# Eight copies of each row of combine weights in memory, and one broadcast transfer for a pair of experts in place of two

## What is computed

```python
logits = x @ router_w.T + expert_bias[None, :]
probs = jax.nn.sigmoid(logits)
top_w, top_idx = jax.lax.top_k(probs, TOP_K)                     # 8 of 160
top_w = top_w / (jnp.sum(top_w, axis=-1, keepdims=True) + 1e-09) * 2.5
combine = zeros((T, 160)).at[jnp.arange(T)[:, None], top_idx].set(top_w)
h1 = jax.nn.silu(jnp.einsum('th,eih->eti', x, w_gate))           # 64 inner columns per expert
h1w = h1 * combine.T[:, :, None]
routed = jnp.einsum('eti,ehi->th', h1w, w_down)
shared = jax.nn.silu(x @ w_gate_shared.T) @ w_down_shared.T
```

## Time and profile before

| what | value |
|---|---|
| median of three runs | 459.23 us (458.0 to 460.93) |
| span of the profiled execution | 459.5 us |
| TensorE busy (matmuls) | 403.9 us, 88% |
| VectorE busy | 332.0 us, 72% |
| ScalarE busy | 305.0 us, 66% |
| GpSimd busy | 239.6 us, 52% |
| moved by SyncE's DMA queue | 77.43 MB, 62.4% of 16 engines' span |
| moved by GpSimd's DMA queue | 10.50 MB, 9.1% |

### The profile page before, as it was taken

How to read it: one execution, slowest core, us unless ns; L and a number is a source line. 1 busy time by engine, 2 the same in 40 slices (tenths; PEclk the granted TensorE clock), 3 DMA queues, 4 the chain that set the end, 5 groups by cost and what they waited for, 6 DMA issues and landing times.

```text
span 459.5 us, 8303 instructions
## 1 busy us (share of the span) xinstructions
PE 403.9 (88%) x2271; PEld 314.5 (68%) x2271; DVE 332.0 (72%) x680; ACT 305.0 (66%) x549; POOL 239.6 (52%) x286
## 2 busy tenths in 40 slices
PE   5876789999999999698999999996999998989973
PEld 3556577878778788476777777775866766666742
DVE  5999879877878899665544444444587978898864
ACT  3258835777768778455666666665468978888861
POOL 2689038877787874133333333200056887888810
PEclk8599989999999999978999999999999999999977
DMA  7100378999989999944564554543999999999932
GB/s 230 51 0 7 91 199 234 273 267 265 258 261 267 258 265 260 303 154 156 163 160 141 150 149 141 142 125 85 344 246 240 238 234 242 242 246 240 219 84 68
DMA packets 46330, 88.37 MB, mean 192 GB/s; under 512 B 17170, under 2 KB 21522, under 8 KB 46292
## 3 DMA queue, kind: packets, MB, share of 16 engines
q1 hardware_dynamic: 40004, 77.43, 62.4%
q0 software_dynamic: 6144, 10.50, 9.1%
q10 hardware_dynamic: 144, 0.00, 0.0%
HBM read 77.79 MB, written 10.10 MB: 191 GB/s over the span
## 4 chain that ended last, share of the span: by engine, by line
PE 42%; DVE 17%; ACT 12%; issue 10%; DMA 10%; POOL 4%; SPq 2%; DVEq 2%; ACTq 2%
PE ps L1496 18%; PE ps L1509 12%; DVE arena L1267 7%; ACT arena L865 7%; PE ps L1518 6%; DMA arena<-combine_scratch 4%; POOL arena L647 3%; DVE ps L1054 2%; PE ps L1666 2%; DMA arena<-expert_rows,row_idx 2%; DMA xn<-combine_scratch 2%; PE ps L1629 1%; DVEq L1267 1%; POOL w_lo L630 1%; DMA x_sb<-x 1%
## 5 line engine op out<-in xcount | busy, mean ns | idle before, releaser
L781 ACT ACTIVATE ps<-ps 128x1024 f32<-128x1024 f32 x80 | 80.9, 1011 | 48.0 <-PE ps L1496 38.7
L1060 DVE TENSOR_TENSOR g_lo<-ps,g_hi 128x1024 fp32r<-128x1024 f32 x81 | 98.3, 1214 | 1.3 <-ACT g_hi L794 1.3
L794 ACT ACTIVATE g_hi<-ps 128x1024 fp32r<-128x1024 f32 x81 | 82.8, 1022 | 15.0 <-DVE ps L1054 12.3
L647 POOL DMA_INDIRECT arena<-expert_rows,row_idx x64 | 61.5, 961 | 58.4 <-issue 57.8
L639 POOL DMA_INDIRECT dispatched<-xn,row_idx x64 | 62.2, 971 | 35.9 <-DVE row_idx L1117 19.0
L1267 DVE COPY arena<-ps 128x128 f32 x112 | 32.7, 292 | 56.8 <-ACT arena L865 43.6
L1054 DVE TENSOR_TENSOR ps<-ps,arena 128x1024 f32<-128x1024 f32 x44 | 54.2, 1232 | 22.2 <-ACT ps L781 12.9
L630 POOL TENSOR_TENSOR w_lo<-w_raw,w_hi 128x384 fp32r<-128x384 f32 x52 | 53.8, 1057 | 29.8 <-ACT w_hi L810 24.0
L1496 PE MATMUL ps<-h_hi,w_hi 128*128 128x512 f32 x162 | 54.3, 416 | 10.7 <-DVE g_lo L1060 5.8
L1509 PE MATMUL ps<-g_hi,w_hi 128*128 128x512 f32 x162 | 53.7, 414 | 5.6 <-ACT g_hi L794 4.6
L1518 PE MATMUL ps<-g_lo,w_hi 128*128 128x512 f32 x162 | 52.8, 408 | 3.9 <-DVE g_lo L1060 3.9
(11 more groups left out here) (216 smaller groups left out, 647.0 us busy)
## 6 DMA issues: line engine op xcount, KB each, us to landing
arena<-combine_scratch SPq DMA_DIRECT2D x88, 256.0 KB
h2T<-combine_scratch SPq DMA_DIRECT2D x48, 256.0 KB
w_raw<-experts SPq DMA_DIRECT2D x27, 384.0 KB
ws<-experts SPq DMA_DIRECT2D x21, 384.0 KB, 3.5
xn<-combine_scratch SPq DMA_DIRECT2D x24, 256.0 KB
expert_rows<-arena SPq DMA_DIRECT2D x16, 256.0 KB, 2.9
xn<-experts SPq DMA_DIRECT2D x6, 384.0 KB, 3.2
arena<-dispatched SPq DMA_DIRECT2D x8, 256.0 KB, 10.1
```

What stands on the lines that cost most here:

```text
L647: pool.indirect_dma_start(out=y_back(n, n + 1), out_offset=None, in_=y_rows[:, :], in_offset=bass.IndirectOffsetOnAxis(ap=row_idx[:, q, k: ...
L781: act.activation(slot(z), slot(z), ACT.Silu).then_inc(silu_done, 1)
L794: act.activation(g_hi[:, k % RING, :].rearrange("p (b n) -> p b n", b=2), slot(z), ACT.Copy).then_inc(hi_ready, 1)
L1060: dve.tensor_tensor(g_lo[:, k % RING, :].rearrange("p (b n) -> p b n", b=2), slot(z), g_hi[:, k % RING, :].bitcast(F32).rearrange("p (b n) ...
```

## The change

The scratch in memory gets eight equal rows for each row of combine weights (COPIES). A store writes every row eight times, from a source that repeats (`store_combine`). A pair then owns sixteen rows of memory, and one transfer takes each of them to eight partitions, 128 in all, 512 KB. EARLY_ROWS is 16 in place of 32; the 34 rows of `combT_b` are stored as 32 and 2. SyncE's wait for the large stores moves from ahead of the turns to the load of pair 8, the first that needs them. The waits on a load count 16 in place of 32.

```diff
-EARLY_ROWS = 32
+EARLY_ROWS = 16
+COPIES = 8
+REST_ROWS = 32
...
-        comb_dram = nc.dram_tensor("combine_scratch", (EC, CHUNK), F32, kind="Internal").ap()
+        comb_dram = nc.dram_tensor("combine_scratch", (EC * COPIES, CHUNK), F32, kind="Internal").ap()
+        comb_rows = comb_dram.rearrange("(e c) n -> e c n", c=COPIES)
...
+            def store_combine(first, end, home, cols):
+
+                src = home.rearrange("e (c n) -> e c n", c=1).to_broadcast((end - first, COPIES, cols.stop - cols.start))
+                return sp.dma_start(comb_rows[first:end, :, cols], src)
+
             def load_combine(pair, s, late=False):
 
-                for n in range(2):
-                    one = comb_dram[bass.ds(2 * pair + n, 1), :]
-                    sp.dma_start(cb_at(s, late)[n * INTER:(n + 1) * INTER, :], one.to_broadcast((INTER, CHUNK))
-                                 ).then_inc(cb_loaded[s], 16)
+                two = comb_dram[bass.ds(2 * COPIES * pair, 2 * COPIES), :].rearrange("(r a) n -> r a n", a=1)
+                sp.dma_start(cb_at(s, late), two.to_broadcast((2 * COPIES, INTER // COPIES, CHUNK))
+                             ).then_inc(cb_loaded[s], 16)
...
             for g in range(GC):
                 sp.wait_ge(combT_a_ready, g + 1)
-                sp.dma_start(comb_dram[0:EARLY_ROWS, tok(g)], combT_a[0:EARLY_ROWS, tok(g)]
-                             ).then_inc(comb_early_stored, 16)
-            sp.dma_start(comb_dram[EARLY_ROWS:P, :], combT_a[EARLY_ROWS:P, :]).then_inc(comb_a_stored, 16)
+                store_combine(0, EARLY_ROWS, combT_a[0:EARLY_ROWS, tok(g)], tok(g)).then_inc(comb_early_stored, 16)
+            everything = slice(0, CHUNK)
+            store_combine(EARLY_ROWS, P, combT_a[EARLY_ROWS:P, :], everything).then_inc(comb_a_stored, 16)
             sp.wait_ge(combT_b_ready, GC)
-            sp.dma_start(comb_dram[P:EC, :], combT_b[:, :]).then_inc(comb_b_stored, 16)
+            store_combine(P, P + REST_ROWS, combT_b[0:REST_ROWS, :], everything).then_inc(comb_b_stored, 16)
+            store_combine(P + REST_ROWS, EC, combT_b[REST_ROWS:EC - P, :], everything).then_inc(comb_b_stored, 16)
             sp.wait_ge(comb_early_stored, 16 * GC)
             for pair in range(1, RING):
                 load_combine(pair, pair)
-            sp.wait_ge(comb_a_stored, 16)
-            sp.wait_ge(comb_b_stored, 16)
...
                         sp.wait_ge(gated, j + 1)
+                        if k + RING == EARLY_ROWS // 2 and not late:
+                            sp.wait_ge(comb_a_stored, 16)
+                            sp.wait_ge(comb_b_stored, 32)
                         load_combine(j + RING, k % RING, late)
...
-                dve.wait_ge(cb_loaded[j], 32)
+                dve.wait_ge(cb_loaded[j], 16)
```

More of the change, by code:

```diff
@@ L1138, in pair @@
                     use = BODY // RING * i + ahead // RING + 1
-                    dve.wait_ge(cb_loaded[ahead % RING], 32 * (use - (ahead % RING == 0)))
+                    dve.wait_ge(cb_loaded[ahead % RING], 16 * (use - (ahead % RING == 0)))
                     gate(j + 1, ahead % RING, ahead, late)
@@ L1330, in _ @@
             first = BODY * (DRAIN_TURN + 1)
-            dve.wait_ge(cb_loaded[0], 32 * (first // RING))
+            dve.wait_ge(cb_loaded[0], 16 * (first // RING))
             gate(first, 0, 0, True)
```

## The result

The changed kernel took 475.88 us (median of four runs, 474.23 to 479.5) beside 460.08 for the kernel before on the same chip: ratio 1.039, 95% interval 1.034 to 1.044. It is 15.8 us slower; the prediction was 465, with a range up to 473, so the sign was right and the size was not. All times given are medians of all runs, while the ratios are taken from the fast runs alone, those within 1.5% of the fastest of their kernel, which is why a ratio can differ from that of two medians.

What follows compares the result with a forecast made beforehand. TensorE was taken to bound the first dense stage, combine loads its two ends, GpSimd the last dense stage. Profiled 459.5 + 10 (stores) - 4.4 (stage end) = 465.1, median 0.3 lower: 464.8, say 465 us; range 456 to 473.

Steps and rivals of the forecast that it cites:

- I take 370, near the upper row: Combine loads: one transfer to 128 partitions runs at 370 GB/s, between 246 (no gain) and 408.
- the term of -4.4: End of the first dense stage: 3.4 us from punctual gates plus 1 us of TensorE clock, 4.4 us less.
- the 3.4 for a punctual gate 44: End of the first dense stage: faster loads remove the 3.4 us by which pair 44's gate is late.
- the 1 behind it: After the first dense stage: 1 us of TensorE's half-clock loss comes back, bounds 0 and 3.4.
- The share of 0.70: First dense stage: the DMA engines' busy share falls from 0.96 to some 0.70.
- the sum had 10: Start: eightfold stores ahead of pair 1's load move its gate later by 10 us, between 7.0 and 13.8.
- a faster load only moves the waits: Last dense stage: GpSimd sets the pace, so faster loads gain nothing there.
- ScalarE's pause of 4.12 us: Pause before 441.50 us: may be DMA's, 0 to 4.1 us less; taken as 0.
- the last stage was DMA's: Rival, 347 to 439 us: loads, not GpSimd, set the pace; gain 14.1 us with the pause, 451 us; chance 0.12.
- late bound of the stores: Start: slowest store rate moves pair 1's gate 13.8 us, giving 468.6; in a rival group of chance 0.16.
- slow small stores: Start: stores from 16 and 32 partitions take 2.6 us more, giving 467.4; in a rival group of chance 0.16.
- loads that stay at 246: Combine loads stay at 246 GB/s, so the 4.4 us are not won: 469.2; in a rival group of chance 0.16.

Runs made afterwards that it cites:

- e1: Kernel before with only the change's load shape (sixteen neighbouring rows, eight partitions each, one transfer), stores as before: 457.64 us, ratio 1.000.
- e3: Kernel before with each load one transfer of 16 groups of 8 distinct expert-weight rows, stores as before: 454.71 us, ratio 0.988.
- e4: Kernel before with the change's load shape, its sixteen rows 36 KB apart in the experts' array: 456.03 us, ratio 0.988.
- e5: Changed kernel with its eightfold stores but the two 64-partition loads of the kernel before: 477.18 us, ratio 1.038 against the kernel before.
- e6: Changed kernel with the loads of pairs 1 and 2 issued ahead of the large stores: 474.89 us, ratio 1.037 against the kernel before.
- e9: Changed kernel's stores with four copies of each row, and the two 64-partition loads of the kernel before: 464.17 us, ratio 1.004 against the kernel before.
- e10: Kernel before with each of its two half loads reading 64 distinct expert-weight rows, stores as before: 460.65 us, ratio 1.002.
- e2: Kernel before with each load one transfer of 128 distinct neighbouring expert-weight rows to 128 partitions: 446.67 us, ratio 0.971.
- e11: Kernel before with one row of combine weights sent to all 128 partitions in one transfer, stores as before: 446.7 us, ratio 0.974.
- e17: Kernel before with one row sent in two 64-partition transfers, to even and odd partitions instead of lower and upper half: 447.76 us, ratio 0.977.
- run 418: Not a run's label: the words are "a plain run 418 GB/s", the rate of sixteen engines on a plain run of rows, 298 to 299.5 us.

## Why the prediction was wrong, step by step

**Right.** The mechanism of the loss: the chain runs from the early store through the large stores to the load of pair 1, and that load is behind them in SyncE's queue. The dense stage hides nothing of it and gives nothing back: TensorE sets its pace, and from gate 1 the steady pace follows 12.84 us later (79.17 to 92.01), 12.55 before, so TensorE's restart cost 0.3 at most, within the 0 to 1 I allowed, with a granted clock of 0.50 (1.2 GHz) from 72 to 78. The pace of the last stage held too: the gates from the tenth to the 34th of it come at 9.62 us for three pairs before and 9.64 after, though GpSimd, forecast to be without a gap, waited 2.2 us in it.

**Wrong, the rate of the loads.** "I take 370, near the upper row": 245 was measured, at a share of 0.90. The row of 408 GB/s had two properties, 128 partitions and distinct sources, and I took the change to share both. It has 128 partitions and sixteen sources, but neither is what counted: the row was a plain run, the change is sixteen groups. Of the term of -4.4, the 3.4 for a punctual gate 44 became 0.6, with that gate as late as before; the 1 behind it stands beside 1.1, which can't come from punctual gates, as there were none. The step behind it was sound: with loads that are really faster, from gate 1 to gate 44 it is 124.3 us (distinct rows), 123.5 (one row for all) and 125.0 (even and odd), 5.5 to 7 less than 130.54. Some 3.4 of that lie in the last three pairs, as forecast; the other 2 to 3.7 lie ahead of them, where TensorE was to hide the gain entirely. The share of 0.70 was too low even so; fast loads leave 0.84.

**Wrong, the size of the start.** The landing was put at 16.4 to 23.2 us after the second early store; it came after 25.5 (53.67 to gate 79.17), so 16.2 of the 18.0 us come from the stores, where the sum had 10, and 1.8 from the stages ahead. By the stretches above: to the end of the early store some 3.8 us, the store of 112 rows 10.1 (3.67 MB at 363), that of 32 rows 4.4 (1.05 at 241), and then 7.2 until pair 1 had landed. At the better mean rate, 375 GB/s, I had 0.7 + 1.4, 9.8, 2.8 and 1.4. The large store was right; the two stores from few partitions cost 3.3 us more, and the last step 5.8 more. In that last step, 72 to 78 us, the engines moved 1.5 MB at 246 GB/s, which is the end of the small stores, the loads of pairs 1 and 2 and weights together: pair 1 was not through before the others had run beside it. Its sixteen completion marks in the trace lie from 71.86 to 77.65 us, eight of them by 74.63, and the last at 79.15, so the engines had drifted 7.3 us apart and the gate waited for the last. The stores of 32 and 2 rows leave nineteen marks, sixteen and three, as transfers on all engines and on two do, and the last of them is at 76.16, 1.9 us behind the next. So the store of two rows did stay on two engines, which only the late bound of the prediction counted, with up to 1.9 us. How much of the 5.8 is that store, and how much the drift of the others, is not shown.

The kernel before had this in small: its store of 34 rows leaves three marks, at its issue, 58.98 and 59.38, and pair 1's last four of 32 come at 60.08 to 61.14, the others by 59.13. With distinct rows, fourteen of pair 1's sixteen marks are in by 58.20 us and the last two at 60.12 and 60.19. The start of before was thus itself some 2 us late for a small store on two engines; no run here splits it otherwise with the rest left as it was.

The rule of the Trainium skill that the prediction weighed (SBUF — State Buffer, Door 1: The DMA port swizzle) agrees with the two small stores: the estimates from it were 2.4 and 4.8 us, and the rows give 3.0 (0.26 MB at 88 GB/s) and 4.4. No run stores them from other partitions, so their size isn't told apart from their place. It also bears on the loads: it lets 64 partitions of one half reach as many ports as 32, and the two halves ran at 236 to 246 GB/s whatever they read, and the even and odd partitions, which reach all the ports, better. But it does not settle the sixteen groups, which reach all the ports in the course of one transfer and are slow all the same. That their engines meet on the same ports at the same time would fit; it was only argued, and no run shows an engine's place.

**Wrong, "a faster load only moves the waits".** The last stage was put at nothing, and ScalarE's pause of 4.12 us with it. In the changed kernel the stage is 2.5 us shorter, of which 2.7 lie in its last pairs, where that pause is gone; its loads are no faster, and one trace each doesn't show the cause. Really faster loads take 5.8 us (one row for all, even and odd) to 7.6 (distinct rows) off it, with 9.28 to 9.37 us for three pairs in place of 9.62. GpSimd is as full as before in it: from 339 to 431 us of the even and odd run

```profile
L647 POOL DMA_INDIRECT arena<-expert_rows,row_idx x58 | 57.9, 998 | 16.3 <-issue 16.2
L630 POOL TENSOR_TENSOR w_lo<-w_raw,w_hi 128x384 fp32r<-128x384 f32 x18 | 18.0, 1023 | 4.4 <-ACT w_hi L810 4.3
```

which stand beside the earlier trace rows. Where the gain lies is told by GpSimd's nine splits in the stage. The last before, then the first and the last of the change, then those of the even and odd run:

```profile
424.70 2.00 POOL L630 TENSOR_TENSOR w_lo<-w_raw,w_hi 128x384 fp32r<-128x384 f32 x2
...
362.80 1.99 POOL L639 TENSOR_TENSOR w_lo<-w_raw,w_hi 128x384 fp32r<-128x384 f32 x2 [4.10 <-ACT w_hi L819]
...
442.77 2.00 POOL L639 TENSOR_TENSOR w_lo<-w_raw,w_hi 128x384 fp32r<-128x384 f32 x2
...
338.69 1.99 POOL L630 TENSOR_TENSOR w_lo<-w_raw,w_hi 128x384 fp32r<-128x384 f32 x2 [3.64 <-ACT w_hi L810]
...
416.76 1.99 POOL L630 TENSOR_TENSOR w_lo<-w_raw,w_hi 128x384 fp32r<-128x384 f32 x2
```

From split to split it is 9.70 us before (the first at 347.14), 10.00 in the change, 9.76 with even and odd partitions and 9.62 with distinct rows. So the pace of before was GpSimd's, as forecast, and a faster load does not quicken it. The gain lies behind the last split, where GpSimd no longer sets the pace: from its start to the last gate it is 20.8 us before, 16.6 in the change, 15.2 with even and odd partitions and 14.4 with distinct rows; the gates up to the 34th take in a part of that, hence their 9.28 to 9.37. The trace of before also hid something: in the seven other kernels with halves or sixteen groups (e1, e3, e4, e5, e6, e9, e10) GpSimd waited 1.7 to 6.2 us for ScalarE between its splits, which came 9.93 to 10.48 us apart; with the three fast loads (e2, e11, e17) it waited 0.7 us at most. So with slow loads GpSimd's pace can suffer too; that the loads cause these waits is not shown, only that they go together. About half of what the rival "the last stage was DMA's" promised (14.1) was there to be had by a load that is faster. (That rival's 8.6 us for three pairs came from a count of matmuls; by the gates, 2.77 us apart, it is 8.3.)

**The range.** The rivals had the pieces: late bound of the stores 13.8, slow small stores 2.6, loads that stay at 246. I priced them one at a time, at most two together, 473. All three together give 459.2 + 13.8 + 2.6 = 475.6, and 475.9 was measured. That it meets so closely is luck: the traces have 18.0 more at the start, of which 1.8 are not the stores', and 4.9 less behind it. They were not independent: the few partitions of the small stores and the shape of the load were both, as it seems, questions of how a transfer meets the memory's partitions, and the row that I read for one of them (246 against 408) was the warning for both.

## What to carry to other kernels

Before a transfer is given the rate of a row in the trace, compare its shape with that row's: how its outermost groups fall on the engines and which partitions each fills, not only how many partitions and bytes it has. Copies in memory that make a load's shape better are paid ahead of the first load, on the same queue, and with few buffers the other order of issue tried here did not hide them; stores from another queue were not tried. Price mechanisms that share one cause together when the range is made.

## What the runs showed of the hardware

- A DMA engine moved about 25 GB/s at a full busy share in the fast shapes (two engines 53 GB/s; sixteen on a plain run 418 GB/s from 298 to 299.5 us at a share of 1.03) and 16 to 17 at nearly the same busy share in the slow shapes (246 at 0.98, 245 at 0.90, 236 at 0.92): a busy share near 1 says nothing of the rate.
- One row read for all 128 partitions ran at 377 GB/s; repeated reads of a row in memory cost nothing that these runs show.
- SyncE's issue of the last two of the change's stores took 2.00 and 2.23 us, where a store of before took 0.42. No cost of it shows here, as the loads behind it had to wait for the data anyway.
- A transfer of 34 or of 2 rows ran on two engines (three completion marks and not sixteen), and a load that is split over all sixteen landed with its late ones.
